# Rotary attention with a second norm: the row normalize moves from GpSimd to ScalarE, and the pipeline's lags and orders are set anew

## What is computed

```python
def _layernorm(x, w, b):
    mu = jnp.mean(x, axis=-1, keepdims=True)
    var = jnp.mean((x - mu) ** 2, axis=-1, keepdims=True)
    return (x - mu) * jax.lax.rsqrt(var + EPS) * w + b

q = q * cos + _rotate_half(q) * sin
k = k * cos + _rotate_half(k) * sin
scores = jnp.einsum('bqhd,bkhd->bhqk', q, k) / jnp.sqrt(jnp.float32(D))
p = jax.nn.softmax(jnp.where(causal, scores, -1e30), axis=-1)
y = jnp.einsum('bhqk,bkhd->bqhd', p, v).reshape(B, T, C)
x = x + y @ proj_w
h = _layernorm(x, ln2_w, ln2_b)
logits = h @ router_w
expert_idx = jnp.argmax(logits, axis=-1)
```

## Time and profile before

| what | us |
|---|---|
| median of 3 executions | 2253.36 |
| lowest, highest | 2251.99, 2255.2 |
| the profiled execution | 2254.86 |
| its span in the profile | 2253.1 |
| rotary attention's pipeline: first turn, last copy of logits | 1877.79, 2014.29 |

### The profile page before, as it was taken

One profiled execution on the slowest core, in us unless ns is written; L12 is line 12 of the kernel. 1 busy time (PEld: TensorE's weight loads), 2 busy tenths in 40 slices (PEclk: granted clock), 3 DMA queues, 4 the chain that ended last, 5 costly groups with the idle time before them and its releaser, 6 DMA issues. The chain is left out here.

```text
span 2253.1 us, 32560 instructions
## 1 busy us (share of the span) xinstructions
PE 2045.2 (91%) x11700; PEld 1723.7 (77%) x11700; DVE 1107.6 (49%) x1946; ACT 940.5 (42%) x1916; POOL 721.1 (32%) x777
## 2 busy tenths in 40 slices
PE   7999999999999999999998677899899665857998
PEld 6888888888888888888886455688799454747998
DVE  3333443434344344434435785423477565646775
ACT  4242323323232332424224697322355454535664
POOL 3030200203030120303100397110388143748884
PEclk9999999999999999999999798899999887978999
DMA  4010010101001010200001200410156113436661
GB/s 160 1 57 1 1 56 0 56 0 56 0 11 44 0 56 0 82 0 0 1 1 38 53 36 30 150 38 10 52 199 196 41 47 117 145 126 222 212 216 59
DMA packets 97919, 144.47 MB, mean 64 GB/s; under 512 B 15566, under 2 KB 72816, under 8 KB 97840
## 3 DMA queue, kind: packets, MB, share of 16 engines
q1 hardware_dynamic: 90784, 127.42, 17.5%
q0 software_dynamic: 4928, 12.86, 1.6%
q10 hardware_dynamic: 2128, 3.15, 0.4%
HBM read 109.32 MB, written 12.06 MB: 54 GB/s over the span
## 5 line engine op out<-in xcount | busy, mean ns | idle before, releaser
L584 DVE TENSOR_TENSOR cond_h<-cond_silu,ps 128x512 f32<-128x512 f32 x288 | 198.1, 688 | 697.2 <-ACT cond_silu L495 693.8
L495 ACT ACTIVATE cond_silu<-ps 128x512 f32<-128x512 f32 x288 | 172.8, 600 | 772.1 <-PE ps L414 772.1
L414 PE MATMUL ps<-a_x_hi,cond_w_hi 128*128 128x512 f32 x1152 | 449.8, 390 | 2.0 <-DVE a_x_lo L262 2.0
L414 PE MATMUL ps<-a_x_lo,cond_w_hi 128*128 128x512 f32 x1152 | 449.2, 390 | 0.0
L414 PE MATMUL ps<-a_x_hi,cond_w_lo 128*128 128x512 f32 x1152 | 449.1, 390 | 0.0
L383 POOL TENSOR_TENSOR cond_w_lo<-cond_stage_up,cond_w_hi 128x256 fp32r<-128x256 f32 x144 | 108.6, 773 | 833.6 <-ACT cond_w_hi L476 833.6
L414 PEld LDWEIGHTS ps<-a_x_hi,cond_w_hi 128*128 128x128 f32 x1152 | 216.9, 188 | 47.4 <-DVE a_x_lo L262 2.4
L414 PEld LDWEIGHTS ps<-a_x_hi,cond_w_lo 128*128 128x128 f32 x1152 | 216.9, 188 | 45.3
L414 PEld LDWEIGHTS ps<-a_x_lo,cond_w_hi 128*128 128x128 f32 x1152 | 216.9, 188 | 45.0
L430 PE MATMUL ps<-cond_h_hi,cond_d_hi 128*128 128x512 f32 x576 | 224.5, 390 | 3.4 <-DVE cond_h_lo L552 3.4
L430 PE MATMUL ps<-cond_h_hi,cond_d_lo 128*128 128x512 f32 x576 | 224.1, 389 | 0.0
(11 more groups left out here) (369 smaller groups left out, 4123.7 us busy)
## 6 DMA issues: line engine op xcount, KB each, us to landing
moe_stage_up<-in_L_ffn_expert_wv SPq DMA_DIRECT2D x22, 1024.0 KB, 8.6
typed_stage_up<-in_L_cond_wi SPq DMA_DIRECT2D x11, 1024.0 KB, 5.0
typed_stage_dn<-in_L_cond_wo SPq DMA_DIRECT2D x11, 1024.0 KB
moe_stage_dn<-in_L_ffn_expert_proj SPq DMA_DIRECT2D x11, 1024.0 KB
cond_stage_up<-in_L_cond_Wg SPq DMA_DIRECT2D x7, 1024.0 KB, 5.0
cond_stage_up<-in_L_cond_Wu SPq DMA_DIRECT2D x7, 1024.0 KB, 7.0
cond_stage_dn<-in_L_cond_Wd SPq DMA_DIRECT2D x7, 1024.0 KB, 5.0
hyp_v_now<-hyp_v_blk SPq DMA_DIRECT2D x16, 272.0 KB, 2.3
```

Source lines behind the costliest of these rows:

```text
L414: ins = pe.matmul(up_ps[st % 2][j], w[:, j, k, fs], x[:, k, tok], start=(i == 0), stop=(i == 3 * KC - 1))
L495: act.activation(silu[:, st % 2], up_ps[st % 2][0], ACT.Silu).then_inc(act_done, 1)
L584: dve.tensor_tensor(h[:, st % 2], silu[:, st % 2], up_ps[st % 2][1], ALU.mult).then_inc(up_free, 1)
```

## The change

The normalize of the rows leaves GpSimd's list. ScalarE computes, beside rstd, a column shift = -mean * rstd (two more operations of 128x1) and does the normalize as one Identity activation with rstd as its scale and shift as its bias, as the last phase of its step. h_turn and h_take go from lag 6 to 8, route and keep from 6 to 9, fetch from 1 to 2, bring_x from 4 to 5, store from 6 to 7. The orders on TensorE, ScalarE and VectorE are new. The score's three waits in the loop move from the mix to the last product of route. The longest lag is 9: steps 0 to 11 and 16 to 24 are written out, steps 12 to 15 are in the loop. The waits for tiles that share a bank follow the lags. GpSimd's total no longer waits for the averages and rstd; x2 waits for total of pair i - 2; `lifted` is now awaited by normalize.

```diff
-                       mix=3, y=3, y_turn=4, y_take=4, out=4, fetch=1, bring_sum=3, bring_x=4, x2=4, stats=5, aggr=5, rstd=5,
-                       total=5, norm=5, weigh=5, lift=5, h_turn=6, h_take=6, route=6, keep=6, store=6)
-            order = dict(tensor="y_turn p_turn h_turn out turn mix score route",
-                         scalar="y_take p_take h_take x2 q_blk rstd prob",
-                         vector="clamp stats top aggr k_blk y keep", gpsimd="shift total norm weigh lift",
+                       mix=3, y=3, y_turn=4, y_take=4, out=4, fetch=2, bring_sum=3, bring_x=5, x2=4, stats=5, aggr=5, rstd=5,
+                       total=5, norm=5, weigh=5, lift=5, h_turn=8, h_take=8, route=9, keep=9, store=7)
+            order = dict(tensor="h_turn y_turn p_turn turn out mix route score",
+                         scalar="y_take h_take p_take q_blk x2 rstd prob norm",
+                         vector="stats clamp top aggr k_blk y keep", gpsimd="shift total weigh lift",
...
-                            wait(pe, kept, i - 5)
+                            wait(pe, kept, i + lag["turn"] - lag["route"])
...
-                            wait(pe, h_taken, i - 4)
+                            wait(pe, h_taken, i + lag["turn"] - lag["h_turn"] + 1)
...
-                                if not hyper and not isinstance(i, int) and (hp, j) == (HP - 1, 1):
-                                    score_ready(i + lag["mix"] - lag["score"])
...
-                        wait(pe, q_taken, i + 5 if not isinstance(i, int) else min(i + 5, NP))
+                        behind = i + lag["h_turn"] - lag["turn"]
+                        wait(pe, q_taken, behind if not isinstance(i, int) else min(behind, NP))
...
-                        wait(pe, k_blocked, i + 6 if not isinstance(i, int) else min(i + 6, NP))
+                        behind = i + lag["route"] - lag["turn"] + 1
+                        wait(pe, k_blocked, behind if not isinstance(i, int) else min(behind, NP))
                         for c in range(KC):
+                            if not isinstance(i, int) and c == KC - 1:
+                                score_ready(i + lag["route"] - lag["score"])
...
                         act.wait_ge(out_done, i + 1)
+                        wait(act, totalled, i - 1)
                         wait(act, scaled, i - 1)
...
                     def inverse(i, q, nth):
 
+                        rstd, shift = router.rstd[:, q:q + 1], router.shift[:, q:q + 1]
                         act.wait_ge(averaged, i + 1)
+                        act.activation(shift, router.mean[:, q, 0:1], ACT.Copy, scale=-1.0).then_inc(rstd_steps, 1)
+                        act.activation(rstd, router.mean[:, q, 1:2], ACT.Ln, bias=router.eps[:]).then_inc(logged, 1)
+                        act.wait_ge(logged, i + 1)
+                        act.activation(rstd, rstd, ACT.Exp, scale=-0.5).then_inc(rstd_done, 1)
+                        act.wait_ge(rstd_steps, 2 * i + 1)
+                        act.wait_ge(rstd_done, i + 1)
+                        act.activation(shift, shift, ACT.Copy, scale=rstd).then_inc(rstd_steps, 1)
+
+                    def normalize(i, q, nth):
+
+                        act.wait_ge(rstd_steps, 2 * i + 2)
                         wait(act, lifted, i - 1)
...
+                        act.activation(router.xn[:, q], router.x2[:, q], ACT.Identity, bias=router.shift[:, q:q + 1],
+                                       scale=router.rstd[:, q:q + 1]).then_inc(scaled, 1)
...
-                        pool.wait_ge(averaged, i + 1)
-                        pool.wait_ge(rstd_done, i + 1)
                         wait(pool, lifted, i - 1)
...
-                        pool.tensor_scalar(router.xn[:, q], router.x2[:, q], router.mean[:, q, 0:1], router.rstd[:, q:q + 1],
-                                           ALU.subtract, ALU.mult).then_inc(scaled, 1)
```

More of the change, by code:

```diff
@@ L684, in __init__ @@
         self.res, self.x = sb("res", [P, 2, KC, P]), sb("x", [P, 2, D])
-        self.stats, self.mean, self.rstd = sb("stats", [P, 2, 6]), sb("mean", [P, 2, 2]), sb("rstd", [P, 2])
+        self.stats, self.mean, self.rstd, self.shift = sb("stats", [P, 2, 6]), sb("mean", [P, 2, 2]), sb("rstd", [P, 2]), sb("shift", [P, 2])
         self.x2, self.xn, self.rows, self.hT = sb("x2", [P, 2, D]), sb("xn", [P, 2, D]), sb("rows", [P, 2, 2 * D]), sb("hT", [P, 2, KC, P])
@@ L1052, in attention @@
         eps_set, gathered, averaged, logged, rstd_done = (sem(n) for n in ("eps_set", "gathered", "averaged", "logged", "rstd_done"))
+        rstd_steps = sem("rstd_steps")
         x2_taken, scaled, weighed, totalled, lifted, h_turned, h_taken, routed, kept = (
@@ L1295, in inverse @@
                     def inverse(i, q, nth):
+                        rstd, shift = router.rstd[:, q:q + 1], router.shift[:, q:q + 1]
                         act.wait_ge(averaged, i + 1)
+                        act.activation(shift, router.mean[:, q, 0:1], ACT.Copy, scale=-1.0).then_inc(rstd_steps, 1)
[7 more added lines that the diff above has]
+                        act.wait_ge(rstd_steps, 2 * i + 2)
                         wait(act, lifted, i - 1)
-                        act.activation(router.rstd[:, q:q + 1], router.mean[:, q, 1:2], ACT.Ln, bias=router.eps[:]).then_inc(logged, 1)
-                        act.wait_ge(logged, i + 1)
-                        act.activation(router.rstd[:, q:q + 1], router.rstd[:, q:q + 1], ACT.Exp, scale=-0.5).then_inc(rstd_done, 1)
+                        act.activation(router.xn[:, q], router.x2[:, q], ACT.Identity, bias=router.shift[:, q:q + 1],
+                                       scale=router.rstd[:, q:q + 1]).then_inc(scaled, 1)
                     def h_take(i, q, nth):
@@ L1311, in _ @@
                         act.wait_ge(eps_set, 1)
-                    run(act, "scalar", dict(x2=take_x2, rstd=inverse, h_take=h_take, q_blk=take_q, root_sq=root_square, root_ln=root_log, root=root, dist_ln=dist_log, dist=dist, prob=exponential, p_take=p_take, y_take=y_take))
+                    run(act, "scalar", dict(x2=take_x2, rstd=inverse, norm=normalize, h_take=h_take, q_blk=take_q, root_sq=root_square, root_ln=root_log, root=root, dist_ln=dist_log, dist=dist, prob=exponential, p_take=p_take, y_take=y_take))
                 @block.vector
@@ L1422, in total @@
                         wait(pool, stored[q], 16 * nth)
-                        pool.wait_ge(averaged, i + 1)
-                        pool.wait_ge(rstd_done, i + 1)
                         wait(pool, lifted, i - 1)
                         pool.tensor_tensor(router.rows[:, q, D:], router.x2[:, q], router.x[:, q], ALU.add).then_inc(totalled, 1)
-                    def normalize(i, q, nth):
-                        pool.tensor_scalar(router.xn[:, q], router.x2[:, q], router.mean[:, q, 0:1], router.rstd[:, q:q + 1],
-                                           ALU.subtract, ALU.mult).then_inc(scaled, 1)
                     def weigh(i, q, nth):
@@ L1446, in _ @@
                         pool.wait_ge(router.loaded, 16 * len(router.loads))
-                    run(pool, "gpsimd", dict(root_add=root_add, mask=mask, shift=shift, total=total, norm=normalize, weigh=weigh, lift=lift))
+                    run(pool, "gpsimd", dict(root_add=root_add, mask=mask, shift=shift, total=total, weigh=weigh, lift=lift))
         sem.give_back()
```

## The result

The changed kernel takes 2228.74 us, median of 4 executions (2227.21 to 2232.7), beside 2254.17 for the kernel before; the ratio is 0.989, with a 95% interval of 0.9876 to 0.9904. That is 25.4 us faster. The forecast was 2232.5, 20.8 us faster, with a range of 2228 to 2242. The profiled execution was the longest of the four, 2232.7 with a span of 2230.9, so the two spans differ by 22.2 only.

What follows compares the result with a forecast made beforehand. A closed two-step chain through GpSimd's lift and TensorE's turn of the normalized rows, about 14.3 us, was taken to set the pitch. Body -11.4, head -0.4 and run-out -9.0 gave -20.8: 2253.36 to 2232.5 us, range 2228 to 2242.

Steps and rivals of the forecast that it cites:

- The 9.0 us of waits for lift: Rotary attention's body: TensorE's 9.0 us over 11 steps, waiting for GpSimd's lift before h_turn, would go.
- TensorE itself: Body: TensorE's own work as the new pitch, 6.03 us in a written-out step, 6.5 in the loop.
- Steps 6 to 8 bound by rounds at 5.75: Body steps without h_turn or route before the score: bound by the rounds, 5.75 us each, 17.3 together.
- The two-step round of 11.3: Body: score through exponential, p_turn, out, mix and route to the next score but one, 11.3 us, 5.65 a step.
- Normalize 0.6, copies 0.25 each: ScalarE: the new normalize takes 0.6 us, bounds 0.39 and 0.81; two added 128x1 copies take 0.25 each.
- rival (d): ScalarE: moved normalize swaps activation tables, two 1.283 us loads per row; slower, 2267 us; chance 0.04, 0.01 for smaller loss.
- SP's steps at nothing: SP queue: later fetch, bring_x and store cost nothing; earlier residual removes step 5's 0.57 wait, gives -0.4 in the head.
- The run-out at 21.5: Last score to last logits' copy: 21.5 us instead of 31.3, plus 0.8 for three added steps; -9.0.
- rival (b): Run-out gives nothing: three more steps of round trips behind the last lift eat the 9.0; 2241.5 us; chance 0.1.
- Rival (a): Body bound by ScalarE's round, not TensorE: pitch 6.6 in the 11 steps from 6 on; 2237 us; chance 0.17.
- (c): New loop wait of about the old size, from SP's transfers or lift; only the run-out gains; 2250 us; chance 0.05.
- (e): The moved turn isn't what TensorE waited for; something just behind it holds as long; no change, 2253 us; chance 0.03.

Runs made afterwards that it cites:

- lags_old_orders: Changed kernel with its lags, but the earlier orders on TensorE, ScalarE (normalize last) and VectorE, and the score's waits back in the mix; 2236.02 us, ratio 0.9917.
- orders_old_lags: Changed kernel with its orders, but h_turn, h_take, route and keep back at lag 6; 2272.11 us, ratio 1.0081 against the kernel before.
- norm_alone: Kernel before, with its lags and orders, and only the normalize moved from GpSimd to the end of ScalarE's step; 2252.89 us, ratio 0.9985.
- waits_in_mix: Changed kernel with the score's three waits put back ahead of the mix's last pair in the loop; 2229.75 us, ratio 0.9882 against the kernel before.
- turn_behind_out: Changed kernel with TensorE doing out ahead of turn, so turn stands right before mix; 2232.4 us, ratio 0.9899 against the kernel before.
- sp_undone: Changed kernel with fetch, bring_x and store back at lags 1, 4 and 6; 2232.24 us, ratio 0.9893 against the kernel before.
- norm_twice: Changed kernel doing the normalize twice on ScalarE, first into a tile that nothing reads; 2234.32 us, ratio 0.9902 against the kernel before.

## Why the prediction was right, and where a term was off

The forecast's mechanism held, and the time, 3.8 us below it, lies inside the range near its lower end. The body's gain was 17.0 where 11.4 was forecast, and the run-out's 9.4 where it was 9.0. Point by point:

- *The 9.0 us of waits for lift go.* Right. No such row is left in the body. None is in lags_old_orders either, and with lag 6 again 1.8 to 2.0 a step are back (orders_old_lags), while the normalize alone leaves 0.63 a step (norm_alone): the lags do it.
- *TensorE itself: 6.03 in a written-out step, 6.5 in the loop.* This is the term that was mis-sized: 5.83 in a written-out step, 5.82 to 5.91 in the loop. I took the distances of starts in the earlier trace rows for work. The mix's 1.21 held 0.15 of waiting for k_blk (1.06 in the changed kernel), and the 0.28 that I put down to three waits on registers in the loop came of the same waiting, with the mix's last product left behind it, and not of issue time: the rows under waits_in_mix show it, and that run and turn_behind_out bear it out. The 0.2 that I added for route rested on a miscount as well: by the kernel one product of two stands ahead of the waits in route, and 15 of 16 stood ahead of them in the mix, not three matmuls and 31 pairs. And the sum took 6.15, 6.55 and 6.1 where the working gives 6.03 and 6.5, 0.6 in all that no row backs. With all this the loop's four steps alone came out 2.7 too long. Over the body: steps 5 to 8 took 21.2 and not 22.9, 9 to 11 took 17.5 and not 18.4, 12 to 15 took 23.5 and not 26.2, step 16 took 5.8 and not 6.1; that is the 5.6 of difference.
- *Steps 6 to 8 bound by rounds at 5.75.* Too long: 5.52, 5.16 and 5.44, 5.37 on average. The two-step round of 11.3 had 0.7 for route in it, and these steps have no route, as the prediction itself says; without it the round is 10.6, or 5.3 a step. In the changed kernel the round from the score at 1906.71 to that at 1917.39 is 10.68: 6.85 to p_turn, where I had 6.6, and 3.83 from there, where I had 4.7.
- *The second round, through keep, mask and k_blk, was not in the prediction at all.* With the old orders the loop stays at 6.5 to 6.9 (lags_old_orders). The forecast gave the new orders no price of their own; they are worth 3.6 to 3.8 us of body over the lags (71.81 to 68.21 and 67.98) and 1 of the run-out. That it didn't spoil the forecast is luck: the prediction never listed this round, and the orders of the change happen to open it.
- *Normalize 0.6, copies 0.25 each.* The groups of the changed kernel, with mean ns:

```profile
L1315 ACT ACTIVATE router_xn<-router_x,router_shift,router_rstd 128x256 f32<-128x256 f32 x16 | 9.4, 589 | 0.1
...
L1309 ACT ACTIVATE router_shift<-router_shift,router_rstd 128x1 f32<-128x1 f32 x16 | 4.7, 295 | 1.5
...
L1303 ACT ACTIVATE router_shift<-router_mean 128x1 f32<-128x1 f32 x16 | 3.1, 195 | 0.0
...
L1325 ACT ACT_TABLE_LOAD x1 | 1.3, 1283 | 0.8 <-PEq L86 0.8
```

  0.589, 0.295 and 0.195. There is one table load in the stage, so rival (d) fell. The Trainium skill (ScalarE: Activation LUTs, "Table sets") has identity in every set, and exp and ln together in one of them; the trace agrees, with this one load of 1283 ns for the whole stage.
- *SP's steps at nothing, -0.4 and -0.6 for the residual.* The cover held, and by the profile the move was worth more than that: 4.1 to 4.3 in the body by sp_undone, since without it the shorter steps would have outrun the residual. I priced what the wait cost at the old pitch, not at the new one.
- *The run-out at 21.5, and 0.8 for the added steps, 22.3.* 21.96. Right within 0.4, but by two errors that partly cancel: the chain was 0.46 too short (x2 of the last row comes 13.6 after the last score, forecast 13.4, and 8.4 follow it, forecast 8.1), and the added steps cost nothing, as the last h_turn 0.06 behind the last lift shows. So rival (b) fell.
- *Rival (a), ScalarE's round.* Not the limit, but near: norm_twice puts its slack at about 0.5 a step.
- *Rivals (c) and (e), a new wait or another one behind the old.* Neither: TensorE's waits from 1905 to 1970 come to 0.2 us.

## What to carry to other kernels

A distance of two starts in a trace is work and waiting together. Before it is used as an engine's floor, hold it against the same phase where its input is surely there, or ask for each phase which late tile stands right behind its maker; a wait in the middle of a group can be listed as "issue". When a pipeline's pitch is a closed round, list all rounds, each engine's own list included, because opening the longest leaves the pitch at the next (here 6.5 to 6.9, through a 4-column copy at the end of VectorE's list), and check the order of a step's phases as carefully as the lags: with the wrong lags the same orders made a kernel 0.8% slower.

## What the runs showed that I had not expected

- A wait for a late k_blk in the middle of the mix is shown as "issue" of 0.18 to 0.87 us, with no releaser named.
- With 1.8 to 2.0 us of idling in front of h_turn, TensorE's clock was at its lower level of 1.2 GHz in the first part of every second step and at 2.4 GHz else (p_turn 1.91 or 1.04 us, orders_old_lags); in the kernel before, with 1.22 us at most there, it stayed at 1.00.
- The same kernel had its clock back 12 us after the first turn in one execution and only within 16 to 20 in another, 2.8 us apart in the head.
- ScalarE's activation with a scale and a bias column at 256 wide takes 0.589; the 128x1 copy takes 0.195 with constants and 0.295 with a column as its scale.
